# Attention kernel: softmax rows transposed by VectorE in 32x32 blocks inside SBUF, value products in eight array tiles

## The reference

```python
xn = ln(x, g_norm)
q = (xn @ Wq).reshape(b, n, HEADS, DIM_HEAD).transpose(0, 2, 1, 3)
kv = xn @ Wkv
k, v = (kv[..., :DIM_HEAD], kv[..., DIM_HEAD:])       # plus the null key and value in front
sim = jnp.einsum('bhid,bjd->bhij', q, k) * SCALE + attn_bias
sim = jnp.where(causal, neg, sim)
attn = jax.nn.softmax(sim, axis=-1)
out = jnp.einsum('bhij,bjd->bhid', attn, v)
return ln(out.transpose(0, 2, 1, 3).reshape(b, n, HEADS * DIM_HEAD) @ Wout, g_out)
```

## Time and profile before

| what | value |
|---|---|
| time, median of 3 runs | 2250.94 us (2246.36 to 2251.7) |
| span of the profiled execution (first to last instruction) | 2243.8 us |
| its own time, beside the span | not listed apart; the median of the runs lies 7.1 us above the span |
| PE busy | 1965.3 us, 88% of the span |
| DVE busy | 1693.1 us, 75% |
| ACT busy | 1338.8 us, 60% |
| POOL busy | 1085.5 us, 48% |
| the three `attend` phases | about 400 to 854, 1010 to 1461 and 1715 to 2175 us |

### The profile page before, as it was taken

One profiled execution on the slowest core, in us unless ns is written; L12 is line 12 of the kernel. 1 busy time (PEld: TensorE's weight loads), 2 busy tenths in 40 slices (PEclk: granted clock), 3 DMA queues, 4 the chain that ended last, 5 costly groups with the idle time before them and its releaser, 6 DMA issues. The chain is left out here.

```text
span 2243.8 us, 46782 instructions
## 1 busy us (share of the span) xinstructions
PE 1965.3 (88%) x11698; PEld 1421.4 (63%) x11698; DVE 1693.1 (75%) x4092; ACT 1338.8 (60%) x2911; POOL 1085.5 (48%) x1307
## 2 busy tenths in 40 slices
PE   5999585999999998589999999985796999999988
PEld 4887463666666668566666666675564666666658
DVE  4777867877887785758777877758577888877857
ACT  2222665777776674247676767644565777766754
POOL 0443222666765562306666666623034666666643
PEclk8999697999999999799999999997896999999999
DMA  4630166333333343286777888830464433333333
GB/s 118 203 109 31 42 226 250 104 113 113 113 114 113 106 149 110 82 312 189 236 241 236 244 244 243 271 142 21 148 229 163 131 115 116 108 115 107 107 113 113
DMA packets 220535, 338.75 MB, mean 151 GB/s; under 512 B 25766, under 2 KB 102700, under 8 KB 220364
## 3 DMA queue, kind: packets, MB, share of 16 engines
q1 hardware_dynamic: 220364, 336.85, 47.3%
HBM read 250.62 MB, written 102.91 MB: 158 GB/s over the span
## 5 line engine op out<-in xcount | busy, mean ns | idle before, releaser
L1653 POOL TENSOR_SCALAR at_row<-at_row,at_inv 128x129 f32<-128x129 f32 (+7 forms) x384 | 715.2, 1862 | 352.9 <-DVE at_inv L1817 347.2
L1864 ACT ACTIVATE at_row<-at_row,at_nmax 128x129 f32<-128x129 f32 (+7 forms) x768 | 595.4, 775 | 231.8 <-DVE at_nmax L1836 230.2
L1836 DVE CUSTOM_DVE_ANT_0 at_row<-at_s,bias,at_row 128x128 f32<-128x128 f32 (+7 forms) x768 | 617.8, 810 | 63.3 <-PE at_s L1764 35.9
L1776 PE MATMUL at_t<-ident,at_row 128*128 128x128 f32 x3456 | 543.9, 280 | 42.6 <-ACT at_pt L1857 37.7
L1776 PEld LDWEIGHTS at_t<-ident,at_row 128*128 128x128 f32 x3456 | 391.4, 141 | 247.9 <-issue 165.7
L1763 PE MATMUL at_s<-k_hh,q_hl 128*128 128x512 f32 (+3 forms) x1152 | 462.2, 401 | 41.9 <-SPq L1721 21.8
L1792 PE MATMUL at_o<-at_pt,v 128*64 128x512 f32 (+3 forms) x2304 | 438.9, 503 | 5.8 <-ACT at_pt L1857 2.5
L1668 DVE COPY at_pt<-at_t 128x128 f32<-128x128 f32 (+3 forms) x576 | 278.5, 484 | 179.6 <-PE at_t L1776 175.7
L1764 PE MATMUL at_s<-k_lp,q_h 65*128 65x512 f32 (+3 forms) x1152 | 392.9, 353 | 0.0
L1857 ACT ACTIVATE at_pt<-at_t 128x512 f32<-128x512 f32 (+2 forms) x576 | 306.7, 533 | 135.5 <-PE at_t L1776 130.3
L1763 PEld LDWEIGHTS at_s<-k_hh,q_hl 128*128 128x128 f32 x1152 | 224.6, 195 | 76.1 <-DVE at_nmax L1836 32.2
(11 more groups left out here) (249 smaller groups left out, 2863.9 us busy)
## 6 DMA issues: line engine op xcount, KB each, us to landing
q_hl<-q_dram SPq DMA_DIRECT2D x192, 256.0 KB, 4.0
q_dram<-o_in SPq DMA_DIRECT2D x76, 512.0 KB, 3.7
bias<-bands_dram SPq DMA_DIRECT2D x64, 512.0 KB, 5.4
q_h<-q_dram SPq DMA_DIRECT2D x96, 256.0 KB, 4.8
o_dram<-o_sb SPq DMA_DIRECT2D x96, 256.0 KB, 4.3
bands_dram<-brow_dram SPq DMA_DIRECT2D x2, 8192.0 KB, 33.6
bias<-corners_dram SPq DMA_DIRECT2D x256, 64.0 KB, 4.2
bias<-in_fside SPq DMA_DIRECT2D x32, 448.0 KB, 4.8
```

The costliest lines, as they stand in the source:

```text
L1653: return eng.tensor_scalar(cells, cells, inv[:, i:i + 1], None, ALU.mult)
L1776: last = eng.transpose(t_ps[m % NTR][:, c * P:(c + 1) * P], row[:, u % RING, here:here + P], t["ident"][:])
L1836: eng.tensor_tensor_reduce(out=row[:, u % RING, ZERO:ZERO + width], in0=s_ps[u % 2][:, 0:width], in1=bt[:, lo:lo + width], scale=-1.0, sca ...
L1864: eng.activation(cells, cells, ACT.Exp, scale=-1.0, bias=nmax[:, i:i + 1], accum_out=rsum[:, i:i + 1]).then_inc(s["exp"], 1)
```

## The change

The transposes by PE, their PSUM buffers and their copies go. In their place DVE transposes a whole row with one instruction, in blocks of 32x32: each of the four groups of 32 partitions is turned within itself. After it, partition 32a+k holds key k of a block of 32 keys for the queries 32a to 32a+31 of the tile (`turned`). The value products follow that layout: array tile (a, side) has 32 rows (keys) and 64 columns (outputs of one head), takes its weights and moving data from the partitions 32a to 32a+31, and writes to a PSUM bank of its own for each a. For each block b of 32 keys there are 8 products, one in each array tile, with up to 4 x 32 = 128 moving columns. So that every group of 32 partitions holds all the keys' values, `project` stores v to DRAM and `attend` loads it back four times (`v_blocks`, 16 DMAs of 128 KB for each layer). The normalization of the even units goes from DVE to ACT. `turned` of the even groups lies in the buffer `q_out[1]`, so the second chunk of outputs for `close_layer` is loaded later. DVE waits once for the stored queries.

```diff
+QG, QGROUPS = 32, 4
@@ project, SP @@
+                    if q % NPAIR == 2:
+                        c = q // NPAIR
+                        eng.wait_ge(s["v_out"], c + 1)
+                        eng.dma_start(t["v_dram"][c * BANK:(c + 1) * BANK, :].rearrange("(n p) d -> p n d", p=P),
+                                      t["v"][:, c * CT:(c + 1) * CT, :]).then_inc(t["v_stored"], 16)
@@ new @@
+def load_value_blocks(eng, t, sem, blocks):
+    for n, block in enumerate(blocks):
+        rows_of = block.shape[1] * QG
+        for a in range(QGROUPS):
+            eng.dma_start(block[a * QG:(a + 1) * QG, :, :],
+                          t["v_dram"][n * rows_of:(n + 1) * rows_of, :].rearrange("(b k) d -> k b d", k=QG)).then_inc(sem, 16)
@@ attend @@
-    NTR = 3
-    VALUES_AT = (0, 2, 4)
+    VALUES_AT = ((1, 4), (0, 2, 4, 6))
+    KEYS_IN_PART = 8
-        t_ps = [ps(f"at_t{n}", [P, BANK]) for n in range(NTR)]
-        o_ps = ps("at_o", [P, BANK])
+        o_ps = ps("at_o", [P, QGROUPS, BANK])
@@ SP @@
+                eng.wait_ge(t["v_stored"], t["v_stored_n"])
+                load_value_blocks(eng, t, s["v_in"], v_blocks)
-                load_first_outputs(eng, t, 1)
                 for g in range(NGRP):
                     store(place(B - 1, TURNS), g - NGRP)
+                    if g == 2:
+                        load_first_outputs(eng, t, 1)
@@ PE @@
-                def transposes(turn, u):
...
                 def values(turn, g, part):
+                    turn.wait(eng, "turned", GU * (g + 1))
                     turn.wait(eng, "out", g)
-                    for j, side in products[cut[part]:cut[part + 1]]:
-                        i0 = max(0, j - (blocks - 4)) * P
-                        last = eng.matmul(o_ps[side * DH:(side + 1) * DH, i0:BANK], t["v"][:, turn.half_of(GU * g) * NT + j, :],
-                                          pt[g % 2][:, side, at + i0:at + BANK], start=j == 0, stop=j == blocks - 1)
+                    for b in range(part * KEYS_IN_PART, (part + 1) * KEYS_IN_PART):
+                        at = max(0, b // QGROUPS - g % 2 * GT) * QG
+                        for a in range(QGROUPS):
+                            for side in range(2):
+                                last = eng.matmul(o_ps[side * DH:(side + 1) * DH, a, at:GT * QG], value_rows(half, b, a),
+                                                  turned[g % 2][a * QG:(a + 1) * QG, side, b, at:GT * QG],
+                                                  start=b == 0, stop=b == key_groups(g) - 1)
@@ DVE @@
+                eng.wait_ge(t["q_stored"], t["q_stored_n"])
+                def transposes(turn, u):
+                    turn.wait(eng, ("norm_a", "norm_p")[u % 2], u // 2 + 1)
+                    turn.wait(eng, "pv", u // GU - 1)
+                    eng.transpose(turned[u // GU % 2][:, u % 2, 0:width // QG, at:at + QG],
+                                  row[:, u % RING, ZERO:ZERO + width].rearrange("p (b i) -> p b i", i=QG)
+                                  ).then_inc(s["turned"], 1)
                 def step(turn, n, has):
-                    if has(n - LAG - 1, U):
-                        evacuate(eng, turn, n - LAG - 1, eng.tensor_copy, 1, "ev_d")
-                    if n % 2 == 1 and has(n, U):
-                        normalize_even(turn, n - 1)
+                    if has(n - LAG, U):
+                        transposes(turn, n - LAG)
@@ ACT @@
+                def normalize_even(turn, u):
+                    turn.wait(eng, "inv", u // 2 + 1)
+                    copy(cells(u), cells(u), scale=inv[:, u % RING:u % RING + 1]).then_inc(s["norm_a"], 1)
                 def step(turn, n, has):
-                        evacuate(eng, turn, n - LAG - 1, copy, 0, "ev_a")
                         exponent(turn, n + 1)
+                    if n % 2 == 1 and has(n - 1, U):
+                        normalize_even(turn, n - 1)
```

More of the change, by code:

```diff
@@ L1607, in attend @@
     n_bias = HP * 2 if toeplitz else U
[L1609 to L1628, removed]
+    GT = NT // 2
+    assert U % NBIAS == 0 and U % RING == 0 and NGRP % 2 == 0
+    marks = dict(qk=U, biased=U, exp=U, inv=U // 2, norm_a=U // 2, norm_p=U // 2, null_in=U // 2, null_out=U // 2, turned=U,
+                 pv=NGRP, out=NGRP)
+    names = list(marks) + ["q0", "q1", "gate", "wo_in", "wo_hi", "wo_lo", "o0", "o1", "v_in"] + [f"bias{n}" for n in range(NBIAS)]
     def slot_loads(n):
@@ L1766, in logits @@
                     last.then_inc(s["qk"], 1)
-                def transposes(turn, u):
-                    turn.wait(eng, ("norm_d", "norm_p")[u % 2], u // 2 + 1)
-                    for m in range(first(u), first(u + 1)):
-                        old = m - NTR
-                        turn.wait(eng, ("ev_a", "ev_d")[old % 2], old // 2 + 1)
-                        at, blocks = pieces[m % NPC]
-                        for c in range(blocks):
-                            here = ZERO + (at + c) * P
-                            last = eng.transpose(t_ps[m % NTR][:, c * P:(c + 1) * P], row[:, u % RING, here:here + P],
-                                                 t["ident"][:])
-                        last.then_inc(s["tr"], 1)
@@ L1780, in values @@
                 def values(turn, g, part):
-                    m = first(GU * (g + 1))
-                    turn.wait(eng, "ev_a", m // 2)
-                    turn.wait(eng, "ev_d", m // 2)
+                    turn.wait(eng, "turned", GU * (g + 1))
                     turn.wait(eng, "out", g)
-                    blocks = 4 * (g % 2) + 4
-                    products = [(j, side) for j in range(blocks) for side in range(2)]
-                    n = len(VALUES_AT)
-                    cut = [k * blocks // n * 2 for k in range(n + 1)]
@@ L1789, in values @@
[L1789 to L1794 removed]
+                    half = turn.half_of(GU * g)
@@ L1795, in values @@
+                    if (part + 1) * KEYS_IN_PART == key_groups(g):
                         last.then_inc(s["pv"], 1)
                 def step(turn, n, has):
-                    u = n - LAG
-                    if has(u, U):
-                        transposes(turn, u)
                     if has(n + 3, U):
                         logits(turn, n + 3)
+                    u = n - LAG
                     g = u // GU - 1
-                    if u % GU in VALUES_AT and has(g, NGRP):
-                        values(turn, g, VALUES_AT.index(u % GU))
@@ L1807, in _ @@
-                start(eng, s, marks, "qk", "tr", "pv")
+                    if u % GU in VALUES_AT[g % 2] and has(g, NGRP):
+                        values(turn, g, VALUES_AT[g % 2].index(u % GU))
+                    if turn.known() and turn.half == 0 and turn.turn < 0 and n == U + LATE - 1:
+                        eng.wait_ge(s["v_in"], 16 * QGROUPS * len(v_blocks))
+                start(eng, s, marks, "qk", "pv")
                 run_halves(eng, step, place, TURNS, U, EARLY, LATE)
@@ L1826, in add_bias @@
                     turn.wait(eng, "null_in", u // 2 + 1)
-                    turn.wait(eng, "tr", first(u - RING + 1))
+                    turn.wait(eng, "turned", u - RING + 1)
                     turn.wait(eng, "qk", u + 1)
```

66 lines of the change are left out of this document (29 added, 37 removed).

## The result

The changed kernel takes 2564.7 us (median of 4, 2560.8 to 2574.3) against 2249.4 us before (2246.4 to 2251.7): ratio 1.140, 95% interval 1.137 to 1.143. I had forecast 2218 with a range of 2140 to 2440. It is slower, by 315 us, and outside the range. The profiled execution has a span of 2559.9 us.

What follows compares the result with a forecast made beforehand. PE was taken as the bound, 27.0 of 28.4 us a pair. From 2250.9 us, -91 for the halves, +38 clock, +15 instruction fetch and +5 later output load gave 2218 us; range 2140 to 2440.

Steps and rivals of the forecast that it cites:

- the main unknown: PE in `attend`: issuing a pair's 768 weight loads and 768 matmuls, taken as nothing, hidden behind 0.213 us of columns.
- 12 jumps: PE's loop: if the longer body leaves the core, each jump back waits 1.2 us for a packet, +15 us.
- a step of 128 columns: PE's values: eight products at 128 columns overlap in eight tiles and take 0.213 us; 0.107 with 64 or 32 columns.
- The clock: PE after a pair's slack second half: lower clock reaches into the first half, 0.8 us a pair, +38 us.
- the clock stays low: Rival: PE at half clock through the slack half, 2.6 us a pair, +125 instead of +38: 2305 us; 19%.
- The sum of the halves: Longer of PE and DVE in each half of a pair, plus 1.4: 26.5 us against 28.4, -91 us.
- both takers absent: Rival: no clock loss on PE and its loop fetched ahead: 2165 us; 12%.
- Transposes at half rate: Rival: DVE transposes at half the copy's rate, 9.6 us more a pair, +384: 2600 us; 6%.
- Issue sets the step: Rival: PE's instruction issue makes a step 0.34 us: 2425; 2515 if row groups load weights one after another; 18%.
- DVE waiting mostly for `at_s`: Trace sign in `attend` that the forecast would be wrong: DVE's waits mostly for that buffer; no size given.
- holes on PE of microseconds: Trace sign that the forecast would be wrong: PE gaps of microseconds at the loop's start.
- a clock of 0.5: Trace sign that the forecast would be wrong: clock at 0.5 for long stretches.

Runs made afterwards that it cites:

- e2: Changed kernel with four blocks of keys in each value product (512 columns, a quarter of the value instructions; output not attention's): 2280.0 us.
- e5: e2 plus matmuls of 512 columns, whose results nobody reads, added behind the logits where PE idles: 2203.4 us.
- e6: Changed kernel, output unchanged, with the same added matmuls as e5: 2562.5 us.
- e16: e14 with 60 instead of 304 always-met waits ahead of the third layer's loops, nothing else changed: 2309.3 us.
- e14: Changed kernel with PE's loop over one pair a turn, e5's added matmuls, and always-met waits ahead of the loops of layers 1 and 3: 2441.7 us.
- e3: Changed kernel with all its value instructions, but products after the first block of keys take only 32 columns (output not attention's): 2603.9 us.

## Why the prediction was wrong, step by step

- **The step that failed: what the instructions cost.** I set "the main unknown", 768 loads and 768 matmuls a pair, to nothing for PE's issue and 15 us for "12 jumps". The first half was right: a step of 128 columns at full clock is 0.221 us (median of 603), 0.21 forecast; one of 32 columns 0.152 against my 0.107, still only 9.5 ns for a load with its matmul. By the 25 ns that I quoted from the Trainium skill (TensorE: Matmul & The Clock Gate, section "Wait — 56ns, not 53.3ns?") it would be 0.40; the trace refutes that for eight tiles. The second half was wrong in kind. I priced a packet for each jump; but a body of 209 KB is fetched anew all the way through, 7 packets a pair, and at PE's own pace: 256 instructions run in 2 us and arrive in 3.3 at best. Slack elsewhere did not make up for it. Measured by e2: 285 us. The stops within parts are 185; no run splits up the rest (waits behind them, stops elsewhere, and 23 us more outside the stretches from first to last bias addition). I had the rows for it: 60 packets before, 200 KB of body; what I lacked was the rate.
- **The clock.** Mis-sized: +38 us taken, 77 measured (e2 less e5). The trace of before had a lower stretch of 3.4 us; here they last 10.2 us and reach through the steps in which PE is the bound, as the rival "the clock stays low" had it (125 us). In the changed kernel itself a higher clock gains nothing, since fetching sets the pace (e6).
- **The sum of the halves.** Too low, too. A pair without fetching and near full clock takes 26.91 us (e5). That must be set beside the 28.04 of the same measure before, and not beside 28.4, which is the length of the phases by 48: the gain is 1.1 us, and 1.9 was forecast. From first to last bias addition the three phases take 1341 us before and 1285 in e5, 56 less instead of 91; outside of them e5 needs 10 us more, 5 were forecast. That is the 38 us by which e5 lies above the 2165 of "both takers absent". DVE's busy share there is 84%, 85 forecast. 285 - 15 for the instructions, 77 - 38 for the clock and these 38 are 347, the whole miss, 2565 - 2218.
- **Right:** DVE's transposes (1.04 ns a column, 1231 ns at 1024), ACT's normalization (1136 ns at 1025 columns), the loads of v, which nothing waits for.
- **The rivals.** Transposes at half rate (2600) lay nearest in time, and the 1.04 ns a column refute them. "Issue sets the step" (2425 to 2515) had the right engine and the right quantity, the number of instructions, but not the mechanism: 1536 resident value instructions a pair take no longer than 384 (29.0 and 28.9 us), and with the clock held up about 0.5 us longer (27.7 in e16, 27.2 in e5). No rival had the packets' rate.
- Of what the trace was to show, "DVE waiting mostly for `at_s`" and "holes on PE of microseconds" came true of the wrong side, and in part "a clock of 0.5": 16.5 of 34 us a pair. The holes are in the parts, wherever a packet ends, and only seldom at the loop's start. Of the right side the step (0.22 us) and the transpose came true; PE, and not DVE, has the largest busy share in `attend`.

With every loop resident and the clock held up (e16) the changed kernel takes 2309 us. Its 30 pairs without a packet take 27.7 us each; the same 30 pairs take 28.6 before. The 104 packets left fall on first turns and on the code between the loops: the nine pairs with four or more packets take 33.5 us each, 52 us more than as many resident ones, and outside the stretches from first to last bias addition e16 needs 40 us more than before (943 against 903, up to 16 of them for the added waits themselves). So the change as made gains 0.9 us in a resident pair and loses it again elsewhere; none of the versions with attention's output beats the kernel before.

## What to carry to other kernels

Count an engine's instructions per microsecond, not only their columns: 24 value products and 72 transposes a pair (120 weight loads with their matmuls in the trace) became 384 small products (768 in the trace); the values kept their columns, and yet it cost 14%, because 256 instructions (one packet) ran faster than the next packet came. Look at the instruction queue's packets in the profile, and at idle time put down to "issue" in mid-group; keep a hot loop's body well below 7 packets (3.1 to 4.2 stayed everywhere; 6.6 stayed or not by a shift of some 120 instructions, e14 and e16). An engine that is made less busy may run at half clock in the place where it is needed: e5 added matmuls and gained 3%.

## What I had not expected of the hardware

- A load and its matmul can follow the pair before in 9.5 ns (32 columns, eight tiles) to 13.8 ns (128 columns), and a stream of them outruns its fetch: 2.5 us (median) from a packet's start to the next instruction, one packet in 3.3 us at best where PE waits for each.
- Waits that are always met, ahead of a loop, change the time by far more than they last: 244 of them less (13.5 us) made e14's 2441.7 into e16's 2309.3, by moving the loop against the packets.
- PE's records filled 92% of e3's first phase, and the granted clock was 0.50 all through it; in e2's, with its records at 83%, it was 0.81.
